# One attention written out step by step with score products alternating between row halves, and a new order of the work before the main loop

## What is computed

```python
amp  = abs(rfft(x, axis=1))                                  # 188 frequencies
src  = concat([x[:, -1:], amp], 1) + pos_encoding            # 189 tokens, 64 wide
a    = mha(src)              # 8 heads, 8 wide: softmax(q k^T / sqrt(8)) v, then out_w
src  = layer_norm(src + a);  src = layer_norm(src + relu(src @ w1.T + b1) @ w2.T + b2)
tau  = clip(softplus(mha(src)[:, -1:]) / 10, 0.01, 1.0)      # second attention, last token
h    = sliding window of 32 rows of x, weighted by powers of tau
h    = h + retention(layernorm(h))                           # rotary Q, K, decay mask
h    = h + product_key_attention(layernorm(h))               # 8 heads, top 16 of 64 x 64 keys
```

## Time and profile before

| | us |
|---|---|
| median of 3 runs (lowest, highest) | 1988.75 (1987.87, 1991.08) |
| the profiled execution, its own time | 1989.92 |
| its span in the trace | 1988.1 |
| PE busy | 1904.1 (96%) |
| DVE, ACT, POOL busy | 1619.4 (81%), 1471.2 (74%), 1323.1 (67%) |
| mean granted clock of PE | 0.979 |
| first attention, first score product to last output taken | about 39 to 137 |
| main loop | about 257 to 1988 |

### The profile page before, as it was taken

One profiled execution on the slowest core, in us unless ns is written; L12 is line 12 of the kernel. 1 busy time (PEld: TensorE's weight loads), 2 busy tenths in 40 slices (PEclk: granted clock), 3 DMA queues, 4 the chain that ended last, 5 costly groups with the idle time before them and its releaser, 6 DMA issues.

```text
span 1988.1 us, 43774 instructions
## 1 busy us (share of the span) xinstructions
PE 1904.1 (96%) x11398; PEld 1488.2 (75%) x11398; DVE 1619.4 (81%) x4827; ACT 1471.2 (74%) x2977; POOL 1323.1 (67%) x1584
## 2 busy tenths in 40 slices
PE   5985799999999999999999999999999999999997
PEld 3973467777777777777777777777777777777776
DVE  3655678888888888888888888888888888888885
ACT  2662377778778777877877787787777778777785
POOL 1220357777777777777777777777777777777774
PEclk9996889999999999999999999999999999999998
DMA  3000010002000200001000200010000200020001
GB/s 106 1 0 26 30 56 20 20 20 62 18 16 19 63 20 20 20 18 59 15 20 20 63 20 16 17 60 20 20 20 20 62 16 15 19 63 20 20 18 27
DMA packets 118088, 57.91 MB, mean 29 GB/s; under 512 B 109696, under 2 KB 116032, under 8 KB 116733
## 3 DMA queue, kind: packets, MB, share of 16 engines
q1 hardware_dynamic: 115250, 56.75, 11.0%
q10 hardware_dynamic: 2795, 0.70, 0.2%
HBM read 24.55 MB, written 0.70 MB: 13 GB/s over the span
## 4 chain that ended last, share of the span: by engine, by line
PE 74%; issue 8%; POOL 7%; DVE 1%; ACT 0%; POOLq 0%; DMA 0%; SPq 0%; DVEq 0%; ACTq 0%
PE ps L968 25%; PE ps L976 14%; PE ps L959 13%; PE ps L980 7%; PE ps L1018 4%; POOL k_W_low L1351 4%; PE ps L1036 3%; PE ps L953 2%; PE ps L1028 2%; PE ps L1003 2%; PE ps L990 1%; PE ps L996 1%; POOL k_aS L1293 1%; PE ps L1019 0%; POOL k_ecs L1337 0%
## 5 line engine op out<-in xcount | busy, mean ns | idle before, releaser
L1517 DVE SCALAR_TENSOR_TENSOR k_W<-ps,k_W 128x688 f32<-128x688 f32 x1028 | 893.3, 869 | 229.8 <-ACT k_W L1161 210.2
L1351 POOL TENSOR_TENSOR k_W_low<-k_W,k_W_high 128x688 fp32r<-128x688 f32 x513 | 850.9, 1659 | 331.6 <-ACT k_W_high L1166 331.6
L1161 ACT ACTIVATE k_W<-ps 128x688 f32<-128x688 f32 x1029 | 766.2, 745 | 363.6 <-PE ps L959 354.0
L968 PE MATMUL ps<-k_W,k_tab 128*128 128x344 f32 x2048 | 677.0, 453 | 0.0
L959 PE MATMUL ps<-k_X,sel 128*128 128x344 f16 x2058 | 471.8, 311 | 9.3 <-DVE k_W L1517 8.8
L968 PEld LDWEIGHTS ps<-k_W,k_tab 128*128 128x128 f32 x2048 | 366.7, 190 | 127.9 <-issue 0.9
L1166 ACT ACTIVATE k_W_high<-k_W 128x688 fp32r<-128x688 f32 x513 | 395.6, 771 | 0.0
L976 PE MATMUL ps<-k_W_high,k_tab_high 128*128 128x344 f32 x1024 | 385.1, 378 | 0.0
L976 PE MATMUL ps<-k_W_high,k_tab_low 128*128 128x344 f32 x1024 | 324.3, 319 | 0.0
L959 PEld LDWEIGHTS ps<-k_X,sel 128*128 128x128 f16 x2058 | 176.7, 99 | 179.0 <-issue 77.6
L980 PE MATMUL ps<-k_W_low,k_tab_high 128*128 128x344 f32 x1024 | 244.7, 320 | 0.1
(11 more groups left out here) (225 smaller groups left out, 2359.8 us busy)
## 6 DMA issues: line engine op xcount, KB each, us to landing
k_tab<-in_tables SPq DMA_DIRECT2D x9, 2048.0 KB, 7.2
k_X<-k_spl SPq DMA_TRANSPOSE x390, 2.3
k_xs<-x2T SPq DMA_DIRECT2D x33, 172.0 KB, 2.1
k_qT<-k_qs SPq DMA_DIRECT2D x33, 86.0 KB, 2.0
cst<-in_consts SPq DMA_DIRECT2D x1, 1024.0 KB, 19.7
wts<-in_weights SPq DMA_DIRECT2D x1, 896.0 KB, 12.9
cst<-in_consts SPq DMA_DIRECT2D x1, 874.5 KB, 17.5
xr<-in_xrows SPq DMA_DIRECT2D x1, 750.0 KB
```

The lines of the kernel that those rows point to most:

```text
L968: mm = mm_(sums, tab[:, slot, at + k, :], W[:, d % RING, k, :], start=(d == 0 and k == 0), stop=(d == NDC - 1 and k == 1))
L1161: A(W[:, d % RING, :, :], ps[:, 2 * (d % 2):2 * (d % 2) + 2, 0:LOUT], ACT.Exp).then_inc(e_done, 1)
L1351: G.tensor_tensor(W_low[:, q % SPLIT_RING, :, :], W[:, d % RING, :, :], W_high[:, q % SPLIT_RING, :, :].bitcast(F32), ALU.subtract).then_i ...
L1517: V.scalar_tensor_tensor(W[:, d % RING, :, :], ps[:, 2 * (d % 2):2 * (d % 2) + 2, 0:LOUT], 0.0, W[:, d % RING, :, :], ALU.is_ge, ALU.mult) ...
```

## The change

1. The first attention is written out as straight code of 32 steps for every engine; nothing is done for a pair after the last.
2. `qz` holds each head once, for both batches (`heads` is the sum of the two batch masks). A score product reads only the 64 rows of its batch from `qz` and from `kT`; `kp` and POOL's copies are gone. The four products of a step still alternate between the batches, so between row halves 0 to 63 and 64 to 127, and between two PSUM banks.
3. values(k - 1) stands in every step from 1 on, the last step of a pair is like the others, and the second inversion of a pair moves into step 2 of the next pair.
4. The output product and the mean of group 0 wait only for pairs 0 and 1. The feed-forward products go by group, and the second product of group 0 waits for four ReLUs.
5. Before the main loop the similarities of round 1 and the turning of `hT` move ahead of the second variance, `copy_similarities(1)` and the copies to `y` move up on ACT, and `halves(1)` moves ahead of the last `normed` on DVE.

The diff, cut to its core:

```diff
-        qz = sb("qz", [128, 2, 2, H, S])
-        kp = sb("kp", [128, 2, S])
+        qz = sb("qz", [128, 2, H, S])
...
-        heads = sb("heads", [128, 2 * H])
+        heads = sb("heads", [128, H])
...
-                pool.wait_ge(k_ready, 2)
-                feed_keys(0, 0)
...
-                feed_values(0, 0)
-                with pool.Fori(0, NPAIR // 2) as pp:
...
-                        following = (p + 1) % NPAIR
-                        pool.wait_ge(score_done, 8 * p + 1)
+                feed_values(0)
+                for p in range(NPAIR):
+                    if p + 1 < NPAIR:
                         pool.wait_ge(oT_ready, 2 * p + 2)
...
-                def scores(par, t):
+                def scores(k):
+                    p, t = k // 8, k % 8
                     qt, j = t // 4, t % 4
                     q0, n = QT[qt]
                     for hf in range(2):
                         for b2 in range(2):
+                            rows = slice(64 * b2, 64 * b2 + 64)
                             mm = nc.tensor.matmul(ps[0:n, 2 * (t % 2) + b2, hf * S:(hf + 1) * S],
-                                                  qz[:, par, b2, 4 * hf + j, q0:q0 + n], kp[:, par, :], start=True, stop=True)
+                                                  qz[rows, p % 2, 4 * hf + j, q0:q0 + n], kT[rows, p, :], start=True, stop=True)
                     mm.then_inc(score_done, 1)
...
                 pe.wait_ge(qz_ready, 2)
-                pe.wait_ge(kp_ready, 1)
-                scores(0, 0)
-                scores(0, 1)
-                with pe.Fori(0, NPAIR // 2) as pp:
-                    for par in range(2):
-                        p = pp * 2 + par
-                        for t in range(8):
-                            pe.wait_ge(exp_done, 8 * p + t + 1)
-                            if t == 6:
-                                pe.wait_ge(qz_ready, 2 * p + 4)
-                                pe.wait_ge(kp_ready, p + 2)
-                            if t < 6:
-                                scores(par, t + 2)
-                            else:
...
-                            turn_probabilities(8 * p + t, t)
...
-                            if t >= 1:
...
-                        values(8 * p + 7, par, 7)
-
-                pe.wait_ge(oT_ready, 2 * NPAIR + 2)
-                pe.wait_ge(exp_done, 8 * NPAIR + 2)
+                pe.wait_ge(k_ready, 2)
+                scores(0)
...
+                for k in range(8 * NPAIR):
+                    pe.wait_ge(exp_done, k + 1)
+                    if k % 8 == 6 and k + 2 < 8 * NPAIR:
+                        pe.wait_ge(qz_ready, 2 * (k // 8) + 4)
+                    if k + 2 < 8 * NPAIR:
+                        scores(k + 2)
+                    turn_probabilities(k)
+                    if k >= 1:
+                        if (k - 1) % 8 == 0:
+                            pe.wait_ge(vz_ready, 4 * (k // 8) + 4)
+                        if (k - 1) % 4 == 0:
+                            pe.wait_ge(oz_ready, k // 4 + 1)
+                        values(k - 1)
+                values(8 * NPAIR - 1)
+
                 for g in range(2):
+                    pe.wait_ge(oT_ready, (NPAIR + 2, 2 * NPAIR + 2)[g])
                     nc.tensor.matmul(ps[:, 4 + g, 0:2 * S], weight("o1"), oT[:, two[g], :], start=True, stop=True).then_inc(proj_mm, 1)
-                layer_norm(0, x1, res_done, 1, 2)
-                for hf in range(2):
-                    for g in range(2):
+                    pe.wait_ge(res_done, g + 1)
+                    nc.tensor.matmul(ps[:, g, 0:2 * S], const("mean"), x1[:, two[g], :], start=True, stop=True).then_inc(mean_mm, 1)
+                for g in range(2):
+                    pe.wait_ge(sqr_done, g + 1)
+                    nc.tensor.matmul(ps[:, 2 + g, 0:2 * S], const("mean"), sqr[:, two[g], :], start=True, stop=True).then_inc(var_mm, 1)
+                for g in range(2):
+                    for hf in range(2):
                         for b2 in range(2):
                             if b2 == 0 and hf == 0:
                                 pe.wait_ge(ln_done, g + 1)
@@ -360,7 +348,7 @@
                                              x1[64 * b2:64 * b2 + 64, two[g], :], start=True, stop=True).then_inc(ff1_mm, 1)
                 for g in range(2):
                     for b2 in range(2):
-                        pe.wait_ge(relu_done, 8)
+                        pe.wait_ge(relu_done, 4 * g + 4)
...
+                for k in range(8 * NPAIR):
+                    copy_turned(k)
+                    if k % 8 == 6:
+                        invert_sums(k // 8, 0)
+                    if k % 8 == 2 and k > 8:
+                        invert_sums(k // 8 - 1, 1)
+                    if k + 2 < 8 * NPAIR:
+                        act.wait_ge(max_done, k + 3)
+                        exponentials((k + 2) % 8)
+                invert_sums(NPAIR - 1, 1)
...
-                    hf, g, b2 = k // 4, (k // 2) % 2, k % 2
+                    g, hf, b2 = k // 4, (k // 2) % 2, k % 2
...
-                def mask_queries(par, p, b2):
-
-                    q = qT[:, p:p + 1, :] if isinstance(p, int) else qT[:, bass.ds(p, 1), :]
-                    V.tensor_tensor(qz[:, par, b2, :, :], q.to_broadcast([128, H, S]),
-                                    heads[:, H * b2:H * b2 + H, None].to_broadcast([128, H, S]), ALU.mult).then_inc(qz_ready, 1)
+                def mask_queries(par, p, hf):
+
+                    q = qT[:, p:p + 1, :]
+                    V.tensor_tensor(qz[:, par, 4 * hf:4 * hf + 4, :], q.to_broadcast([128, 4, S]),
+                                    heads[:, 4 * hf:4 * hf + 4, None].to_broadcast([128, 4, S]), ALU.mult).then_inc(qz_ready, 1)
...
+                V.tensor_tensor(heads[:, :], const("batch_head")[:, 0:H], const("batch_head")[:, H:2 * H], ALU.add).then_inc(heads_step, 1)
                 dve.wait_ge(heads_step, 1)
+                V.tensor_scalar(heads[:, :], heads[:, :], DH ** -0.5, None, ALU.mult).then_inc(heads_step, 1)
+                dve.wait_ge(heads_step, 2)
...
-                        for t in range(8):
-                            if t == 5:
-                                take_outputs(p, 0)
-                            row_max(8 * p + (t + 2), (t + 2) % 8)
-                            copy_turned(t)
-                            if t in (1, 3):
-                                mask_queries(1 - par, (p + 1) % NPAIR, t // 2)
-                        take_outputs(p, 1)
+
+                def copy_turned(k):
+                    dve.wait_ge(ptr_done, k + 1)
+                    V.tensor_copy(PT[:, k % 2, 0, :], ps[0:95, 4, 0:380]).then_inc(pt0_ready, 1)
+
+                for k in range(8 * NPAIR):
+                    if k % 4 == 1 and k > 1:
+                        take_outputs((k - 4) // 8, (k - 4) // 4 % 2)
+                    if k + 2 < 8 * NPAIR:
+                        row_max(k + 2, (k + 2) % 8)
+                    copy_turned(k)
+                    if k % 8 in (1, 3) and k + 8 < 8 * NPAIR:
+                        mask_queries(1 - k // 8 % 2, k // 8 + 1, k % 8 // 2)
+                take_outputs(NPAIR - 1, 1)
                 dve.wait_ge(bo_ready, 1)
                 for g in range(2):
                     dve.wait_ge(proj_mm, g + 1)
                     V.scalar_tensor_tensor(x1[:, two[g], :], bank2(4 + g), bo[:, :], src[:, two[g], :], ALU.add, ALU.add).then_inc(res_done, 1)
-                layer_norm(0, bias("g1"), bias("b1"))
+                    dve.wait_ge(res_done, g + 1)
+                    centre_tokens(0, g)
+                scale_tokens(0, bias("g1"), bias("b1"))
                 for g in range(2):
                     dve.wait_ge(ff2_mm, 2 * g + 2)
                     V.scalar_tensor_tensor(x1[:, two[g], :], bank2(4 + g), bias("fb2"), x1[:, two[g], :], ALU.add, ALU.add).then_inc(res_done, 1)
-                layer_norm(1, bias("g2"), bias("b2"))
+                for g in range(2):
+                    centre_tokens(1, g)
+                scale_tokens(1, bias("g2"), bias("b2"))
...
                 pe.wait_ge(ln_done, NPAIR + 1)
                 similarities(0, 0, 0)
                 mix(3)
-                for p in range(1, NPAIR):
-                    second_mean(p)
-                    second_variance(p)
-                pe.wait_ge(log_done, 2 * NPAIR)
+                pe.wait_ge(zeroed, 9)
+                pe.wait_ge(ret_done, 3)
+                similarities(1, 1, 0)
+                second_mean(1)
+                pe.wait_ge(ret_done, NPAIR)
                 for t, (t0, m) in enumerate(TT):
                     for p in range(NPAIR):
-                        mm = tr_(ps[0:m, YBANK[t], 128 * p:128 * p + 128], hT[:, p, t0:t0 + m], eye)
+                        mm = tr_(ps[0:m, t, 128 * p:128 * p + 128], hT[:, p, t0:t0 + m], eye)
                     mm.then_inc(y_mm0, 1)
-                pe.wait_ge(zeroed, 9)
-                similarities(1, 1, 0)
+                second_variance(1)
```

(17 more changed lines are left out.)

93 lines of the change are left out of this document (34 added, 59 removed).

## The result

The change makes the kernel slower: the median of four runs is 2027.24 us (2025.51 to 2031.15), beside 1989.32 us for the kernel before, a ratio of 1.0195 (95% interval 1.0181 to 1.0210). The forecast was 1964.3 us. The profiled execution of the changed kernel takes 2028.49 us, its span 2026.7.

A forecast was written before the change was run, and what follows sets the result against it. PE was taken to bound attention and main loop, chains over all engines between them. Gains 18.1 + 1.9 + 4.5 = 24.5 us from 1989.92 gave 1965.4, for the median 1964.3 us; range 1957.5 to 1972.

The forecast's parts named there:

- the low clock: First attention, rival: products on half the rows keep PE at 1.2 GHz, making the kernel slower; chance 3%.
- Its price: Clock rival's time: PE's 77 us of attention work would double, about 2040 us; gain lost at 25 us low.
- Scores: Attention step: row halves overlap, eight passes fill five slots, 0.85 us instead of 1.36, gaining 0.51 a step.
- the price of the change of form: Attention step: three array-form changes instead of two, cost taken as inside the 0.85 us; a drain estimated at 0.05.
- Attention: First score product to last outputs: 81.4 us instead of 98.0, a gain of 16.6, with the start 18.1.
- Between the attentions: First to second attention: group 0's early output work saves 1.0 us, its second feed-forward product 0.9 to 1.1; sum 1.9.
- The filling: Ahead of the main loop: line 980 comes about 4.5 us earlier beyond the other gains, range 2.5 to 7.
- The DMA transposes are no bar: Filling: six start from 242.46 in 7.72 us, third issued at 246.3, so they would not delay the earlier exponentials.
- The search moved ahead: Filling: halves(1) no longer holds DVE and POOL behind the first exponentials, 2.5 us more; PE gives back some 0.5.
- The main loop: From line 980 on: untouched by the change, same length as before; a difference over 1 us would refute the forecast.
- No overlap: Attention scores, rival: row-half products stay one after another; only other parts gain, 1977.7 us; chance 7%.
- half overlap: Attention scores, rival: half overlap or a drain at each form change, scores 1.10 us, step 2.66, 1970.5 us; 11%.

The follow-up runs named there:

- e1_full_rows: Changed kernel with its score products on all 128 rows again, masks wide again: 1979.13 us, ratio 0.9949.
- e5_first_three: Changed kernel with the first three score groups on all 128 rows, later ones on row halves: 1968.53 us, ratio 0.9896.
- e6_from_three: Changed kernel with the first three score groups on row halves, all later ones on all 128 rows: 1982.95 us.
- e11_cut_stretches: e6_from_three with scores and turning of each step cut in halves that alternate: 1981.91 us.
- e7_pair_ends: Changed kernel with the last values group of each pair back in that pair's last step: nine runs 1980.18 to 1983.87 us, one 2014.45.
- e12_twice_halves: Changed kernel with the products of the first three score groups issued twice, all on row halves: 1963.82 us, ratio 0.9872.
- e10_halves_late: e5_first_three with halves(1) on DVE again behind the first four masked weights, not ahead of the last normed: 1972.03 us.
- e4_warm_start: Changed kernel with eight extra 128-row, 378-column products on PE ahead of the first scores: 1965.68, 1966.37, 2027.16 and 2028.98 us.
- e3_batch_order: Changed kernel with both score products of one batch, then both of the other: 2024.61 us.
- e9_plain_four: Changed kernel with the turnings of steps 0 to 3 alone as plain identity products: 1967.38, 1969.14, 1969.16, 1974.22 and 2032.37 us.
- e2_before_halves: Kernel before with only its score products cut to the 64 rows of their batch: 1976.83, 1978.0, 1978.98, 1990.15 and 2024.2 us.

## Why the prediction was wrong, point by point

**The step that failed** is the clock. The prediction read 1.00 in the window from 48.56 us on the earlier trace rows, took it as a property of the attention, and gave the low clock 3%. It did not ask where the clock of before had come from. The trace of before shows it, in PE's windows at the start of the attention:

```profile
39.00:40.00 1.00, 1.00 (x6) 1.00 0.00 0
40.00:41.00 1.00, 1.00 (x6) 0.56 0.00 0
...
42.00:43.00 1.00, 1.00 (x4) 0.50 0.00 0
43.00:44.00 1.00, 1.00 (x5) 0.73 0.00 0
44.00:45.00 1.00, 1.00 (x10) 1.00 0.00 0
```

The clock falls at 40.1 us in the kernel before too, and it rises again at 43.5, in the full-row scores of steps 0 to 2. A row that was on the table held the sign: 24 score instructions begin at 39.00 and the next group at 44.67, 0.24 us each and not 0.17. The change removed both ways back, the full-row products and the ends of pairs, and each alone brings the clock back: by the times of the runs, full-row products in all of them (e1_full_rows, e5_first_three, e6_from_three, e11_cut_stretches), the ends of pairs at once in nine runs of ten (e7_pair_ends). The arguments against this rival were true and beside the point. The retention's 64-row products do run at full rate, but the earlier trace rows show products at a clock that is up already, and keeping it is not the same as getting it.

**Its price** was too high: 2040 forecast, 2027 measured. PE's work does not double: a step takes 4.46 us at low clock beside 2.44 at full clock, 1.8 times. 61.2 us are lost in the attention against e12_twice_halves, not 77. The point from which the gain is lost was named as a third of the attention; here it was all of it, since the clock did not recover in the steady steps in any run of the changed kernel. Two of the prediction's own signs of being wrong came up: a granted clock of the attention under 0.95 (0.51), and a main loop off by more than 1 us (1.8 shorter in the changed kernel, 2.3 in e12_twice_halves).

**At full clock the sum holds.** e12_twice_halves has the attention that was forecast. One step of it, and the end:

```profile
97.73 0.88 PE L283 MATMUL ps<-kT,qz 64*95 64x189 f32 x8
98.55 0.90 PE L294 MATMUL ps<-cst,P 94*95 94x94 f32 x8
99.37 0.87 PE L309 MATMUL ps<-PT,vz 95*64 95x94 f32 x16
100.29 0.88 PE L283 MATMUL ps<-kT,qz 64*95 64x189 f32 x8
...
119.42 0.35 DVE L538 COPY oz<-ps 128x188 f32<-128x188 f32 x1 [1.22 <-PE ps L309]
```

- Scores: forecast 0.85, measured 0.82. The turning behind them takes 0.82 where it was 0.75; the prediction thought the price of the change of form to be inside its 0.85, and 0.07 a step more stands there. That it is a drain is not shown.
- Every fourth step is 2.56 (these rows), the others 2.44. From step 2 to step 29, 45.90 to 115.09 us, 28 steps take 69.2, forecast 69.2. The tail takes 4.3, forecast 4.2.
- Attention 82.2, forecast 81.4. The products issued twice are in it.

**Between the attentions**: forecast 1.9, measured 4.0 (29.5 to 25.5). What was missed is that the output product and mean of group 0 now run while the clock of the attention is still up, 0.90 us each, where both groups took 2.89 and 2.73 at low clock before. The stretch behind it gives 1.9 back, which the forecast had at nothing: the clock falls and rises at other moments, and a retention group of twelve products takes 2.46 and 2.36 us there:

```profile
197.26 2.53 PE L915 MATMUL ps<-k_tab 64*128 64x344 f32 x12 [0.50 <-DVE k_tab L1447]
199.72 2.43 PE L926 MATMUL ps<-k_tab,k_y 128*64 128x344 f32 x12
202.08 1.97 PE L915 MATMUL ps<-k_tab 64*128 64x344 f32 x12
```

Line 915's kind of group took 1.30 at full clock.

**The filling**: forecast 4.5, measured 4.0 in e12_twice_halves and 2.6 in the changed kernel. The total was near, its parts were not. The exponentials do not follow the last `normed` at once, as forecast. "The DMA transposes are no bar" is wrong: the prediction counted when the third is issued, not when it has landed. The changed kernel:

```profile
291.64 0.51 DVE L1427 TENSOR_TENSOR x2T<-k_W 128x344 f32<-128x344 f32 x1
292.14 1.31 PE L955 MATMUL ps<-k_X,sel 128*128 128x344 f16 x4 [1.67 <-DMA k_X<-k_spl]
293.00 1.38 ACT L1161 ACTIVATE k_W<-ps 128x688 f32<-128x688 f32 x2 [1.42 <-PE ps L955]
```

PE waits for them 1.67 us, and ACT 1.42 for PE. The search moved ahead gives 1.0 here and not 2.5 (e10_halves_late).

**The main loop** from its first low sum is 2.3 us shorter in e12_twice_halves, forecast nothing. Of this 1.8 is the second round: the first two low sums of before stand at 261.91 and 266.65, 4.7 apart, those of e12_twice_halves 3.0 apart (238.11 and 241.10). The same products lie between them; in before four of line 968 take 1.99 us to the next start (263.74 to 265.73), in e12_twice_halves 1.15 at full clock. In before the clock is at 1.00 up to the first low sum and at 0.50 from 262.0 to 265.4; in e12_twice_halves it is at 1.00 from the first low sum to the second. By e10_halves_late this belongs to the place of the search, which the prediction priced by POOL's first part alone.

**The other rivals.** No overlap and half overlap are refuted by the 0.82 us. The forecast's 1964.3 us is what the change gives when its clock is kept (1963.82), but the change as made does not keep it, and 1964.3 was the wrong number for it. That the two agree within 0.5 us is in part luck: by stretches the forecast is 2.1 us too high between the attentions and 2.3 in the main loop, and 1.8 too low ahead of the first similarities and 0.8 in the attention, where e12_twice_halves also has twelve products more.

**What is shown and what stays open.** Shown: the loss is the low clock of the attention (same steps at full clock: 1963.8 to 1966.4 us in e4_warm_start and e12_twice_halves), it begins behind PE's wait at the start, and steps with scores on all rows bring the clock back while the changed kernel's own steps did not in any of its runs, nor in those of e3_batch_order. Open: what exactly in a row-half step keeps a low clock low, and how the extra products of e12_twice_halves keep it up. Neither transposes alone (e9_plain_four) nor the length of the stretches (e11_cut_stretches) explains it, and the same stream gave both levels in e4_warm_start and e9_plain_four. Why the four runs of e4_warm_start divide is not settled either, for lack of a trace of the slower ones.

## What to carry to other kernels

Before products are made smaller or thinner, look where the clock of that stretch rises, not at its level in the steady part: the work that lifts it may be the work that the change removes. PE's waits shortly ahead of a long stretch of turnings and thin products are worth a trial with products that compute nothing new: here twelve of them were worth 63 us in four runs of four, while eight larger ones one wait earlier (e4_warm_start) helped in two runs of four. Several executions are needed to judge it. And a forecast that hangs on the clock should carry its two levels as two cases of real weight.

## What the runs showed of the hardware

- PE busy without a pause does not bring the full clock: 117.15 of 117.15 us busy at 0.50 in e9_plain_four. The Trainium skill (TensorE: Matmul & The Clock Gate, Why this matters for your kernels) asks for no long idle gaps between bursts of matmuls. The traces agree for the start, where the clock fell in twelve of thirteen behind a wait of 2.51 or 3.89 us; the absence of gaps was not enough for getting it back.
- The two levels are both stable over a whole attention of row-half steps, 78 us at 1.00 and 140 us at 0.50. In e4_warm_start, e9_plain_four and e2_before_halves the runs of one kernel lie at or near both; what decides is not known.
- Row-half score products of a step take 0.82 us at full clock (e12_twice_halves), where full-row ones take 1.36, and at half clock 1.50 or 1.51 by the order of the batches (changed kernel, e3_batch_order). At full clock the turnings behind them take 0.07 us more than behind full-row ones.
